# Vision tower: the order of TensorE's small products in the preparation of the state-space scan

## The chip, the cores and the metric

The kernel runs on one core of a Trainium2 chip. The metric is the device time of one execution in microseconds (us), the median of several runs. Engines: PE is TensorE, ACT ScalarE, DVE VectorE, POOL GpSimd, SP SyncE, which here only issues DMAs.

## The reference

An image tokenizer turns 128 images into 5 tokens of 256 channels each (h). Then a bidirectional Mamba block and an expert layer follow. For each of two directions d the Mamba block computes, over the 5 tokens:

```
xz = x @ in_w.T;  xi, z = split(xz)                  # 512 + 512 channels
xc = silu(conv_b + causal 4-tap convolution of xi)
dbl = xc @ xproj_w.T;  dt, Bm, Cm = dbl[:16], dbl[16:32], dbl[32:48]
delta = softplus(dt @ dt_w.T + dt_b)
h = exp(delta * A) * h + delta * Bm * xc;  y = h . Cm    # scan over the tokens
y = (y + xc * D_skip) * silu(z) @ out_w.T
```

## The kernel before, in words

The program is one function, `tower`, in four stages: token, preparation, scan, finish. Each engine has its own list of instructions for each stage, written out by hand; engines meet only at semaphores, so the order of the lists is the order of the work, and a wait holds back all that stands behind it on that engine. The change lies in the preparation alone.

Names on PE in the preparation (128 images on the partitions of a result, or channels where it says so):

- `xi(n)`, n = 0 to 7: input projection of one 128-channel part of a direction (0 to 3 forward, 4 to 7 backward), into PSUM. ACT begins the convolution (`conv_begin`), DVE adds the three other taps, ACT ends it with silu (`conv_end`, semaphore `xc_ready`).
- `xp(d, c)`: the projection `xc @ xproj_w.T`, part c of 4, as 5 products with 48 columns. fp32 products run in two passes, so one `xp` is 10 instructions (L1033). The last part lets ACT copy the result to SBUF (`copy_bc(d)`, tile bct), from which all below follows.
- `turn_dt(d)`: 5 transposes of the dt columns (L1041), then ACT's `copy_dt(d)`.
- `spread_c(d)`: 6 transposes (L1047) of the tile cd, in which POOL has spread the C columns over groups (`c_spread(d)`; the tile is single, so POOL fills it for d = 1 only after `spread_c(0)` has read it), then ACT's `copy_cd(d)`.
- `dt_product(n)`, n = 0 to 9: `dt @ dt_w.T + dt_b` for one (direction, token) item, 33 rows by 512 columns, two passes (L1065). Items 0, 1, 2 are forward; item 3 is the first backward one and needs `copy_dt(1)`. In the text these are the delta products.
- `z(n)`, n = 0 to 7: the gate projection of one item, 128 rows by 512 columns, four passes (L1027). `silu_z(n)` on ACT takes it to SBUF (L1167); n = 0 and 1 are only copied there (their silu follows in the last stage).
- `xt(n)`: 4 transposes and 8 passes of diagonal products (L1056, L1058) for item n.

For each item ACT computes exp(-|.|) (`exponential_of(n)`: L1194, L1199), DVE `plus_one` (L1380), `lost` (L1384) and `above` (L1389), ACT the logarithm (L1210), and DVE then forms delta (`delta_`, L1399), u (L1409), and three bf16 parts of both with ACT (`high` L1219, `middle` L1225, `low` L1433). SP stores these parts in DRAM (`store(n)`, L1012), reads them back for the scan, and between `store(1)` and `store(2)` stores the backward B parts (`store_b(1)`, L1561). Items 0 to 4 run through DVE in a fixed front part (`plus_one` of 2 and 3, `lost` of 2 and 3, `above` of 2 and 3, then item 4, then `delta_(0)`); items 5 to 9 are woven in behind that, one `dt_product(n)` for each, released by `above(n - 1)` (`rc_ready`).

PSUM has 8 banks of 512 columns. Banks 2 and 3 hold in turn the backward `xi(5)`, `turn_dt(0)` and `spread_c(0)`; banks 4 to 7 hold delta and gate products.

Of the kernel before, what the change touches and what calls it, by code (L numbers as in the profile page):

```python
# [76 lines left out]
def tower(nc, a, out):  # L77
    top = ExitStack()
    with top:
# [911 lines left out]
        ZS = [8, 3, 1, 7, 2, 4, 5, 6]  # L991
        Z_BANK = [6, 7, 6, 7, 4, 5, 6, 7]
        NEZ = len(EARLY)
# [21 lines left out]
        def prepare_tensor(pe):  # L1015
# [22 lines left out]
            def turn_dt(d):  # L1038
                pe.wait_ge(bct_ready, d + 1)
                for t in range(L):  # L1040
                    mm = pe.transpose(wide(DTT_SLOT[d], t * B, (t + 1) * B, R), bct[:, d, t, 0:R], ident[:, :])  # L1041
                mm.then_inc(dtt_ready, 1)
# [19 lines left out]
            def dt_product(n):  # L1062
                d, t = ITEMS[n]
                pe.wait_ge(dtT_ready, d + 1)
                pe.matmul(bank(DP_BANK[n]), dtT[:, d, t * B:(t + 1) * B], dtw[:, d, :],  # L1065
                          start=True, stop=True).then_inc(dp_ready, 1)
# [24 lines left out]
            dt_product(0)  # L1091
            pe.wait_ge(acc_ready, 7)
            dt_product(1)
            dt_product(2)
            pe.wait_ge(xc_ready, DC + 3)
            xp(1, 2)
            pe.wait_ge(xc_ready, 2 * DC)
            xp(1, 3)
            spread_c(0)
            pe.wait_ge(acc_ready, 2 * DC)  # L1100
            turn_dt(1)
            dt_product(3)
            pe.wait_ge(rc_ready, 1)
            dt_product(4)
# [12 lines left out]
            pe.wait_ge(CT_ready, 2)  # L1117
            z(0)
            pe.wait_ge(rc_ready, 6)
            dt_product(7)  # L1120
            xt(3)
            z(1)
            pe.wait_ge(rc_ready, 7)
            dt_product(8)
            xt(4)
            pe.wait_ge(z_copied, NEZ + 1)
            z(2)
            pe.wait_ge(rc_ready, 8)
            dt_product(9)
            xt(5)  # L1130
            pe.wait_ge(z_copied, NEZ + 2)
            z(3)
            pe.wait_ge(rc_ready, 9)
# [12 lines left out]
        def prepare_scalar(act):  # L1146
# [100 lines left out]
            conv_end(7)  # L1247
            exponential_of(0)
            copy_bc(1)
            b_high(1)  # L1250
            exponential_of(1)
            copy_dt(1)
            exponential_of(2)
            copy_cd(0)
            exponential_of(3)
            exponential_of(4)
# [12 lines left out]
            middle(2)  # L1269
            silu_z(0, ACT.Copy)  # L1270
            softplus_terms(8)
            high(3)
            middle(3)
            silu_z(1, ACT.Copy)
            softplus_terms(9)
# [1021 lines left out]
```

## Time and profile before

| | |
|---|---|
| median of 3 runs | 502.53 us (500.88 to 507.13) |
| the profiled execution: its own time | 500.95 us |
| its span | 499.1 us |
| mean granted clock of TensorE | 0.965 of full speed |
| PE, DVE, ACT, POOL busy | 90%, 75%, 48%, 34% of the span |

The span runs from the first to the last instruction of the profiled execution; 1.85 us lie around it. A granted clock of 1.00 is 2.4 GHz, 0.50 is 1.2 GHz. The preparation lies at about 204 to 290 us of the span.

### The profile page before, as it was taken

What the parts mean: (1) busy time and instruction counts of PE and PEld (TensorE: products, weight loads), DVE (VectorE), ACT (ScalarE), POOL (GpSimd) and SP (SyncE); (2) the same over time, 40 slices, a digit from 0 to 9 for tenths busy, and PEclk for the clock granted to TensorE, in tenths of its full rate; (3) what the DMA queues carried; (4) which work ended last, traced back from release to release, by engine and by line L of the source; (5) the groups of instructions that cost most, each with busy time, mean ns of one, the idle gap of its engine ahead of it and who ended that gap; (6) DMA issues with size and microseconds to landing.
All of it is one profiled execution on the core that took longest, in us unless ns stands there. A gap on an engine that the chain in (4) does not pass through costs nothing.

```text
span 499.1 us, 6891 instructions
## 1 busy us (share of the span) xinstructions
PE 450.0 (90%) x1816; PEld 228.5 (46%) x1816; DVE 372.3 (75%) x709; ACT 238.8 (48%) x422; POOL 168.4 (34%) x164
## 2 busy tenths in 40 slices
PE   6999999999999989899969738988889889799997
PEld 3554655655555567577635402122222222285654
DVE  0256586566666668564999968899999999989756
ACT  1143423112212323365888855788888888531100
POOL 6000100100100020414430014889898989421000
PEclk9999999999999999996699967899999999999999
DMA  8992029200000000312035663466555655530000
GB/s 262 309 292 80 1 91 304 56 1 0 0 2 0 0 1 0 106 54 80 1 96 174 188 184 83 136 173 193 157 152 173 188 163 158 143 90 12 11 12 21
DMA packets 36344, 51.75 MB, mean 104 GB/s; under 512 B 5922, under 2 KB 26926, under 8 KB 36320
## 3 DMA queue, kind: packets, MB, share of 16 engines
q1 hardware_dynamic: 34736, 49.86, 34.0%
q10 hardware_dynamic: 1584, 1.59, 1.0%
q8 instruction: 12, 0.20, 0.2%
q14 instruction: 12, 0.10, 0.1%
HBM read 34.59 MB, written 16.52 MB: 102 GB/s over the span
## 4 chain that ended last, share of the span: by engine, by line
PE 65%; DVE 10%; SPq 8%; DMA 7%; issue 5%; ACT 3%; POOL 1%; DVEq 0%; POOLq 0%
PE ps L325 14%; PE ps L397 12%; PE ps L2085 7%; PE ps L1730 4%; PE ps L2052 4%; DMA brows<-bparts 4%; PE ps L1020 3%; PE ps L1683 3%; PE ps L1033 2%; DMA area<-in_xT 2%; PE ps L1696 2%; SPq L1544 2%; PE ps L1705 2%; PE ps L346 2%; PE ps L1065 2%
## 5 line engine op out<-in xcount | busy, mean ns | idle before, releaser
L1876 POOL TENSOR_TENSOR gb<-da,hb 128x512 f32<-128x512 f32 x62 | 77.7, 1275 | 61.1 <-ACT da L1796 54.2
L1796 ACT ACTIVATE da<-da 128x512 f32<-128x512 f32 x128 | 79.0, 629 | 25.0 <-DVE da L1907 20.9
L1907 DVE TENSOR_TENSOR da<-ps,expA 128x512 f32<-128x512 f32 x128 | 84.1, 685 | 8.0 <-PE ps L1683 7.2
L325 PE MATMUL ps<-area,convw 128*128 128x384 f32 (+1 forms) x220 | 73.4, 486 | 1.2 <-DMA area<-in_xT 1.2
L397 PE MATMUL ps<-wall,peT 128*128 128x512 f32 x144 | 67.7, 593 | 0.0
L1683 PE MATMUL ps<-drows,selb 96*128 96x512 bf16 x128 | 48.5, 401 | 11.7 <-DVE da L1907 5.1
L325 PEld LDWEIGHTS ps<-area,convw 128*128 128x128 f32 (+1 forms) x220 | 41.2, 190 | 29.0 <-DMA area<-in_xT 1.8
L1696 PE MATMUL ps<-urows,brows 96*128 96x512 bf16 x96 | 35.0, 394 | 13.9 <-DVE gb L1914 7.5
L582 ACT ACTIVATE kvs<-ps 128x512 f32<-128x512 f32 x36 | 21.5, 597 | 52.6 <-PE ps L397 52.6
L574 ACT ACTIVATE peT<-ps 128x384 f32<-128x384 f32 x24 | 11.8, 490 | 66.5 <-PE ps L325 59.3
L1683 PEld LDWEIGHTS ps<-drows,selb 96*128 96x128 bf16 x128 | 11.4, 98 | 61.9 <-DVE da L1907 50.1
L1876 POOL TENSOR_TENSOR gb<-da,gb 128x512 f32<-128x512 f32 x30 | 37.8, 1281 | 0.0
L1730 PE MATMUL ps<-gb,cst 128*8 128x512 f32 x256 | 34.0, 603 | 2.4 <-DVE gb L1969 1.5
L2085 PE MATMUL ps<-expw,xfT 128*128 128x512 f32 x76 | 34.2, 598 | 0.0
L688 DVE BATCH_NORM_STATS2 st<-ps 128x6 f32<-128x256 f32 x40 | 16.8, 429 | 21.7 <-PE ps L346 21.7
L397 PEld LDWEIGHTS ps<-wall,peT 128*128 128x128 f32 x144 | 24.5, 190 | 17.2 <-issue 17.2
L287 POOL TENSOR_TENSOR rstd<-veps,mhalf 128x1 f32<-128x1 f32 x4 | 2.2, 551 | 79.0 <-DVE veps L715 79.0
L1696 PEld LDWEIGHTS ps<-urows,brows 96*128 96x128 bf16 x96 | 9.1, 98 | 35.2 <-DVE gb L1914 21.3
L289 POOL TENSOR_TENSOR rstd<-veps,mhalf 128x9 f32<-128x9 f32 x4 | 7.2, 1806 | 51.5 <-DVE veps L736 51.5
L2178 DVE SCALAR_TENSOR_TENSOR mo<-ps,hot,mo 128x256 f32<-128x256 f32 x40 | 19.3, 484 | 5.5 <-PE ps L2085 4.1
L1914 DVE TENSOR_TENSOR gb<-da,ps 128x512 f32<-128x512 f32 x32 | 21.6, 676 | 1.9 <-ACT da L1796 1.9
L2085 PEld LDWEIGHTS ps<-expw,xfT 128*128 128x128 f32 x76 | 13.9, 190 | 14.8 <-issue 14.1
(246 smaller groups left out, 775.4 us busy)
## 6 DMA issues: line engine op xcount, KB each, us to landing
area<-in_xT SPq DMA_DIRECT2D x11, 768.0 KB
yscr<-yst SPq DMA_DIRECT2D x28, 208.0 KB
brows<-bparts SPq DMA_DIRECT2D x16, 240.0 KB, 3.0
drows<-dparts SPq DMA_DIRECT2D x14, 192.0 KB, 2.8
uparts<-pt SPq DMA_DIRECT2D x18, 128.0 KB, 2.4
dparts<-pt SPq DMA_DIRECT2D x18, 128.0 KB, 2.4
urows<-uparts SPq DMA_DIRECT2D x15, 144.0 KB, 2.7
inw<-in_in_wT SPq DMA_DIRECT2D x2, 1024.0 KB
```

The costliest lines, as they stand in the source:

```text
L325: mm = pe.matmul(bank(T_EMB + j % 2, 0, EN), convw[0:n, k, h * P:(h + 1) * P], xbuf[0:n, q, k, c * EN:(c + 1) * EN], start=(k == 0), stop= ...
L397: mm = pe.matmul(bank(T_KV + (q + t) % 2), peT[:, q, h, t * B:(t + 1) * B], wall[:, h, 512:1024], start=(h == 0), stop=(h == CH - 1))
L582: act.activation(kvs[:, q, t, :], bank(T_KV + (q + t) % 2), ACT.Copy).then_inc(kv_free, 1)
L1683: pe.matmul(bank(j % 2), selb[:, j % 2, :], drows[:, q, o:o + DI], start=True, stop=True).then_inc(e_ready, 1)
L1696: mm = pe.matmul(bank(b_), brows[:, q, o * P:(o + 1) * P], urows[:, q, v:v + DI], start=True, stop=lone, skip_group_check=True)
L1730: mm = pe.matmul(ps[32 * j:32 * j + GB, (6 + k) * 512:(7 + k) * 512], cst[:, q, d, token(s_, d), :], gb_at(q, 4 * k + j), start=True, stop ...
L1796: act.activation(da_at(q, j), da_at(q, j), ACT.Exp, scale=-1.0).then_inc(da_ready, 1)
L1876: pool.tensor_tensor(gb_at(q, j), da_at(q, j), state, ALU.mult).then_inc({2: m2_done, 3: m3_done, 4: m4_done}[s_], 1)
L1907: dve.tensor_tensor(da_at(q, j), bank(j % 2), expA[:, j % 2, :], ALU.mult).then_inc(e_free, 1)
L1914: dve.tensor_tensor(gb_at(q, d), da[:, d, :], bank(bu_bank(q, d)), ALU.mult).then_inc(bu_used, 1)
L2052: mm = pe.matmul(bank(2 + n % 2, 0, C), ygT[:, n % 2, d, c, :], outw[:, d, c, :], start=(d == 0 and c == 0), stop=(d == 1 and c == DC - 1))
L2085: mm = pe.matmul(bank(4 + m % 3), xfT[:, n % 2, h, :], expw[:, h, k * 512:(k + 1) * 512], start=(h == 0), stop=(h == CH - 1))
```

## The change

On PE, `z(0)` comes right behind `dt_product(0)`; the last two parts of the backward projection (`xp(1, 2)`, `xp(1, 3)`) come ahead of `dt_product(1)` and `dt_product(2)`; `turn_dt(1)`, `z(1)`, `dt_product(2)`, `dt_product(3)` follow, and `spread_c(0)`, which stood ahead of `turn_dt(1)`, comes behind them and behind a new wait for the copies of both gate products. These two gate products are written to banks 2 and 3 in place of 6 and 7, and since banks 6 and 7 are free, `z(2)` and `z(3)` take the places of `z(0)` and `z(1)` and lose their waits. On ACT the two copies move forward: behind `exponential_of(0)` and behind `exponential_of(2)`; `copy_cd(0)` moves behind `exponential_of(3)`. The work itself is the same: no instruction is added or removed.

```diff
--- before.py
+++ after.py
@@ -989,7 +989,7 @@
         DP_BANK = [4, 6, 7, 5, 4, 5, 4, 5, 4, 5]
         BC_BANK, DTT_SLOT = [4, 5], [1, 0]
         ZS = [8, 3, 1, 7, 2, 4, 5, 6]
-        Z_BANK = [6, 7, 6, 7, 4, 5, 6, 7]
+        Z_BANK = [2, 3, 6, 7, 4, 5, 6, 7]
         NEZ = len(EARLY)
         XI_AT = [1024 * slot + (NE * B if n < DC else 0) for n, slot in enumerate(XI_SLOT)]
         CD_SLOT = [1, 3]
@@ -1089,17 +1089,20 @@
                 xp(1, c)
             pe.wait_ge(cleared, 3)
             dt_product(0)
-            pe.wait_ge(acc_ready, 7)
-            dt_product(1)
-            dt_product(2)
+            z(0)
             pe.wait_ge(xc_ready, DC + 3)
             xp(1, 2)
             pe.wait_ge(xc_ready, 2 * DC)
             xp(1, 3)
-            spread_c(0)
+            pe.wait_ge(acc_ready, 7)
+            dt_product(1)
             pe.wait_ge(acc_ready, 2 * DC)
             turn_dt(1)
+            z(1)
+            dt_product(2)
             dt_product(3)
+            pe.wait_ge(z_copied, NEZ + 2)
+            spread_c(0)
             pe.wait_ge(rc_ready, 1)
             dt_product(4)
             pe.wait_ge(diag_ready, 2)
@@ -1115,21 +1118,17 @@
             dt_product(6)
             xt(2)
             pe.wait_ge(CT_ready, 2)
-            z(0)
+            z(2)
             pe.wait_ge(rc_ready, 6)
             dt_product(7)
             xt(3)
-            z(1)
+            z(3)
             pe.wait_ge(rc_ready, 7)
             dt_product(8)
             xt(4)
-            pe.wait_ge(z_copied, NEZ + 1)
-            z(2)
             pe.wait_ge(rc_ready, 8)
             dt_product(9)
             xt(5)
-            pe.wait_ge(z_copied, NEZ + 2)
-            z(3)
             pe.wait_ge(rc_ready, 9)
             z(4)
             xt(6)
@@ -1246,13 +1245,15 @@
             b_middle(0)
             conv_end(7)
             exponential_of(0)
+            silu_z(0, ACT.Copy)
             copy_bc(1)
             b_high(1)
             exponential_of(1)
             copy_dt(1)
             exponential_of(2)
+            silu_z(1, ACT.Copy)
+            exponential_of(3)
             copy_cd(0)
-            exponential_of(3)
             exponential_of(4)
             for n in range(5):
                 logarithm(n)
@@ -1267,11 +1268,9 @@
             softplus_terms(7)
             high(2)
             middle(2)
-            silu_z(0, ACT.Copy)
             softplus_terms(8)
             high(3)
             middle(3)
-            silu_z(1, ACT.Copy)
             softplus_terms(9)
             logarithm(5)
             high(4)
```

## Rows read from the trace of the kernel before

**Rows 1.** Page, chain of waits, share of the span by engine.
```profile
PE 65%; DVE 10%; SPq 8%; DMA 7%; issue 5%; ACT 3%; POOL 1%; DVEq 0%; POOLq 0%
```

**Rows 2.** Windows (start:end, length; busy us of each engine; then PEclk, DMA).
```profile
228.00:230.00 2.00, 2.00 (x6) 0.81 (x5) 0.36 (x2) 1.97 (x3) 1.39 (x2) 0.78 0.00 0
...
230.00:232.00 2.00, 2.00 (x12) 2.00 (x11) 1.12 (x2) 0.30 (x1) 0.00 (x0) 0.50 0.47 122
...
244.00:246.00 2.00, 2.00 (x11) 2.00 (x10) 1.93 (x4) 2.00 (x5) 0.00 (x0) 0.50 0.00 0
...
246.00:248.00 2.00, 2.00 (x11) 1.35 (x11) 2.00 (x4) 1.11 (x3) 1.44 (x2) 0.95 0.00 0
```

**Rows 3.** Chain of waits in order of time (start us, us, what), 223 to 241.
```profile
223.97 0.55 PE ps L1041 x5
...
224.51 2.17 PE ps L1033 x20
...
226.68 2.96 PE ps L1065 x6
...
229.64 4.43 PE ps L1033 x20
...
234.07 1.31 PE ps L1047 x6
...
235.38 1.08 PE ps L1041 x5
...
237.22 2.09 PE ps L1065 x2
...
240.63 0.43 DVE rc L1380
```

**Rows 4.** Timeline of ACT (start us, us), 229 to 244.
```profile
229.68 0.63 ACT L1199 ACTIVATE ez<-ez 128x512 f32<-128x512 f32 x1
...
234.10 0.37 ACT L1175 ACTIVATE bct<-ps 128x240 f32<-128x240 f32 x1 [3.80 <-PE ps L1033]
...
241.67 0.63 ACT L1199 ACTIVATE ez<-ez 128x512 f32<-128x512 f32 x1
...
243.61 2.71 ACT L1210 ACTIVATE ez<-ez 128x512 f32<-128x512 f32 x5
```

**Rows 5.** Timeline of DVE, 235 to 246.
```profile
235.96 1.38 DVE L1380 TENSOR_SCALAR rc<-ez 128x512 f32<-128x512 f32 x1 [4.46 <-ACT ez L1199]
...
240.97 1.28 DVE L1384 SCALAR_TENSOR_TENSOR rc<-rc,ez 128x512 f32<-128x512 f32 x2
...
245.15 0.68 DVE L1399 TENSOR_TENSOR du<-rc,ez 128x512 f32<-128x512 f32 x1
```

**Rows 6.** Timeline of POOL at its second spread.
```profile
235.52 1.53 POOL L1335 TENSOR_TENSOR cd<-bct,maskb 128x640 f32<-128x640 f32 x1 [6.14 <-PE ps L1047]
...
237.49 0.46 POOL L1340 TENSOR_TENSOR cd<-cbl,maskb 128x128 f32<-128x128 f32 x1
```

**Rows 7.** Timeline of PE, 246 to 273.
```profile
246.11 0.87 PE L1047 MATMUL ps<-ident,cd 128*128 128x128 f32 x6
...
263.54 1.88 PE L1027 MATMUL ps<-inw,area 128*128 128x512 f32 x4
...
266.40 1.12 PE L1065 MATMUL ps<-dtw,dtT 33*128 33x512 f32 x2 [0.98 <-DVE rc L1389]
...
268.84 3.60 PE L1027 MATMUL ps<-inw,area 128*128 128x512 f32 x8
```

**Rows 8.** Timeline of ACT, 260 to 268.
```profile
260.65 0.58 ACT L1167 ACTIVATE area<-ps 128x512 f32<-128x512 f32 x1
...
267.56 0.60 ACT L1194 ACTIVATE ez<-ps 128x512 f32<-128x512 f32 x1 [1.86 <-PE ps L1065]
```

**Rows 9.** Timeline of DVE at 269.
```profile
269.51 0.69 DVE L1384 SCALAR_TENSOR_TENSOR rc<-rc,ez 128x512 f32<-128x512 f32 x1 [0.24 <-ACT rc L1206]
```

**Rows 10.** Timeline of the SP queue, stores of the second B.
```profile
260.74 1.90 SPq L1561 DMA_DIRECT2D bparts<-bhi  x3
```

## The prediction

> **What bounds the kernel now.** The page's chain of waits comes first: PE has 65% of it, over all stages [rows 1], so only the stretch that the change touches matters. The chain in order of time shows that stretch: from 224 to 239.3 us it is PE nearly throughout (turn_dt, four parts of projection, delta products, spread_c, turn_dt again, dt_product(3)), then one exponential on ACT, and from 240.63 DVE [rows 3]. The windows show why PE takes so long there: its clock is granted in full until about 229 us, is 0.50 (1.2 GHz) in the windows between 229 and 246, and is back at 0.95 in 246:248 [rows 2]. The price is in the chain: the same twenty projection passes take 2.17 us at 224.51 and 4.43 us at 229.64; five transposes take 0.55 and 1.08 us [rows 3]. Behind PE the two others starve: ACT idles 3.80 us before the backward copy_bc, which stands ahead of exponential_of(1) in its list, and DVE idles 4.46 us before plus_one(1) [rows 4, 5]. Before the clock fell, PE had done five narrow transposes, twenty passes of 48 columns and six passes of 33 rows: all small. From 245.15 on DVE works on items in a fixed weave, and everything later hangs on when it starts delta_(0) [rows 5].
>
> **The change part by part.** I count to the end of exponential_of(3), since DVE's lost(2) starts behind plus_one(3) at 240.97 and runs on without a gap to delta_(0) at 245.15 [rows 5]; what that exponential gains, DVE gains.
>
> Prices at the full clock: a delta product occupies PE 0.86 us (a gate product has four passes of 512 columns and a delta product two, so half of what follows; with its tail it shows as 1.12 us [rows 7]). A gate product: one takes 1.88 us with its tail, two take 3.60, so each occupies PE 1.72 us [rows 7]. Two projection parts: 2.17 us. turn_dt 0.55 us. spread_c 0.87 us at 246.11 [rows 3, 7]. ACT: an exponential 1.24 us (0.60 and 0.63), a copy of a gate product 0.58 us [rows 4, 8].
>
> PE, with the clock held at 1.00: dt_product(0) starts at 226.68 and ends at 227.55, z(0) at 229.3, the two projection parts at 231.45, dt_product(1) at 232.3, turn_dt(1) at 232.9, z(1) at 234.6, dt_product(2) and (3) at 236.3.
>
> ACT: exponential_of(0) ends at 230.31 as now, table load included [rows 4]. The copy of z(0) ends at 230.9, in time that was idle: cost nothing, and without that cover 0.6. copy_bc(1) waits for the projection and runs 231.5 to 231.9, against 234.10 now; exponential_of(1), behind dt_product(1), 232.4 to 233.65; copy_dt(1) in the wait that follows; exponential_of(2), for which dt_product(2) is ready at 235.5, to 236.75; the copy of z(1) to 237.35; exponential_of(3) to 238.55. Now it ends at 240.60, at the chain's 240.63 [rows 3]. **Gain 2.05 us.** The copy of z(1) lies on this path, so 0.6 us of what the clock gives back is spent there.
>
> What is late next? The new wait before spread_c(0) holds back, on PE, spread_c(0), dt_product(4) and both first xt. It opens at 237.35, spread_c ends at 238.2, dt_product(4) at 239.1, exponential_of(4) at 240.65 against 242.30 now [rows 4]. DVE needs it only after lost and above of items 2 and 3, at 241.4, so it is covered by 0.8 us. The first logarithm ends 1.9 us behind exponential_of(4) (table load, then the first of the five from 243.61 [rows 4]), thus at 242.55, ahead of delta_(0) at 243.1. POOL's second spread also waits for spread_c(0): now it runs from 235.52 to 237.95 [rows 6], then from 238.3 to 240.75 (with the low clock below, half a microsecond later), while PE reaches spread_c(1) behind two xt at about 241.9. Its later B parts wait for ACT's middle of B, as now, and SP stores them at 260.74 behind store(1) [rows 10]; covered.
>
> The second half is less sure. Between the end of z(1) at 234.6 and the first xt at 239.1 PE has only delta products, a wait of 1.1 us and transposes, the mixture before which the clock fell at 229. I take the clock to be at 0.50 there from about 237.5. Then spread_c takes 1.31 us instead of 0.87, and dt_product(4) 2.09 instead of 1.12 with its tail [rows 3, 7]: 1.4 more. exponential_of(4) ends at about 242.05, 0.65 later than DVE wants it, the first logarithm 1.9 later at 243.95, and delta_(0) starts 0.6 to 0.85 behind 243.1: **a cost of 0.7 us**, bounds 0 (clock held) and 1.4 (both in full on the path). xt(0) and xt(1) at the low clock take as long as now and start earlier.
>
> The trace has the clock return at 246 after two xt, each of them transposes and diagonal products [rows 2], so it can't tell which counted. The Trainium skill, page "TensorE: Matmul & The Clock Gate", section "Part 4: PE-mode transpose", states that transposes do not count as work that brings or keeps the full clock. By that rule the stretch behind z(1) falls to 1.2 GHz, which makes the sum -1.35; if the clock holds there, it is -2.05. No row here shows which.
>
> Moved away from later: z(0) and z(1) and their two copies leave the stretch 252 to 266. There PE waits for DVE (0.98 us before the dt_product at 266.40) and ACT for PE (1.86 us at 267.56), while DVE works almost without a gap [rows 7 to 9]; the 1.72 us of PE and 0.58 of ACT for each [rows 7, 8] free nothing that counts: gain 0. The first of the two dropped waits was open before PE came to it (that copy ended at 261.2, z(2) started at 263.54 [rows 7, 8]), and both gate products now sit behind the same products of DVE: gain 0, bound 0.1. From delta_(0) on, DVE, the last items' ACT work, SP's stores and the loads of the scan follow in the same order, so I take the whole shift through to the end.
>
> Sum: -2.05 + 0.7 = **-1.35 us**. On the profiled execution (span 499.1, 1.85 around it): 500.95 - 1.35 = 499.6 us. Its time lies 1.58 under the median of the runs shown; on the median 502.53 - 1.35 = 501.2 us, my forecast.
>
> **The rivals.**
> 1. *The clock falls at 229 as before* (slower). turn_dt, two projection parts and dt_product(0) stand ahead of z(0) unchanged, 3.6 us of small work, and z(0) may come too late for the clock. Then z(0) has just ended, the projection ends at 233.7 as now, dt_product(1) costs 1.7, turn_dt 1.08, z(1) twice 1.72 = 3.44, so PE is through z(1) only at 239.8. With the clock back by then, dt_product(2), its exponential, the copy and exponential_of(3) end at 240.7, 242.1, 242.65 and 243.9: 3.3 us later than now. Time 502.53 + 3.3 = 505.8. It decides from the point where z(1) runs at 1.2 GHz ahead of delta products that ACT waits for. For it: the fall in the rows follows 5.1 us of small products, and only the last 1.5 of these are replaced. Against it: z(0) has every row and 512 columns, as xi has, beside which the clock stayed up.
> 2. *The clock holds through z(0), but falls during the projection, dt_product(1) and turn_dt that follow* (3.6 us of small work). z(1) then costs up to 1.72 more, and the gain shrinks to -0.3: 502.2.
> 3. *Given back later.* Where z(2) stood at 263.54 PE now idles behind xt(4), some 2.9 us until the next delta product [rows 7]. If the clock falls there, dt_product(9) costs 0.86 more; DVE has a gap of only 0.24 left behind the exponential it feeds [rows 9], and ACT is late with all that follows it. 0.6 to 1.0 us lost: about -0.5, 502.0.
>
> **How the numbers follow.** Forecast 0.45, rival 1 0.2, rival 2 0.2, rival 3 0.15. Low end: both terms at their best (-2.1) on the fastest run shown, 500.88, gives 498.8, and 0.5 less for what one run differs from another. High end: forecast, rivals 2 and 3 on the median reach 502.2; the runs before spread upward by 4.6, and half of rival 1 should be in, so 504.5. A change of 2% would be 10 us, about what this measurement can tell from none; no case comes near half of that: faster 0.01, same 0.97, slower 0.02.
>
> **What the profile after would show.** Clock 1.00 in 228 to 232 and projection passes of about 2.2 us for twenty (right), or 0.50 and 4.4 (rival 1). copy_bc(1) near 231.5. exponential_of(3) near 238.6, delta_(0) near 243.8 instead of 245.15. A clock under 1.00 near 238, but back before dt_product(5). At 260 to 268 a clock of 1.00, else rival 3. The first stores of SP and the scan's first products 1.35 us earlier. Wrong would be: delta_(0) earlier, but the scan's start not; that would mean that stores or loads, not DVE, set the scan's start.

## The result and the profile after

The changed kernel takes 503.89 us (median of 20 runs, 500.52 to 506.39), the kernel before 502.33 us (20 runs, 498.71 to 507.13). The ratio is 1.0046, 95% interval 1.0025 to 1.0067: 1.3 to 3.4 us slower. The forecast was 1.35 us faster. The measured time lies inside the stated range, the direction is wrong.

The profiled execution of the changed kernel took 500.52 us (span 498.7), the fastest of all that were timed, so its span is no measure of the change. What lasts in it is the order of events inside the preparation. I count from the start of plus_one(0) on DVE, which is at 230.34 us before and at 230.04 after. The page's chain of waits of the kernel after, share of the span by engine:

```profile
PE 69%; DVE 13%; issue 8%; ACT 3%; SPq 3%; DMA 2%; POOL 1%; DVEq 1%; POOLq 0%
```

PE leads and DVE follows as in [rows 1], so this page doesn't tell what the change did, and its stretch has to be read by itself. The windows of the kernel after (columns as in [rows 2]):

```profile
228.00:230.00 2.00, 2.00 (x12) 1.28 (x11) 0.10 (x1) 1.97 (x4) 1.10 (x1) 1.00 0.00 0
230.00:232.00 2.00, 2.00 (x16) 1.68 (x15) 1.12 (x2) 0.92 (x4) 0.00 (x0) 1.00 0.59 162
238.00:240.00 2.00, 2.00 (x11) 1.07 (x11) 1.06 (x1) 1.80 (x4) 1.16 (x1) 1.00 0.03 8
240.00:242.00 2.00, 2.00 (x12) 2.00 (x11) 2.00 (x3) 1.95 (x3) 1.92 (x4) 0.51 0.01 4
...
252.00:254.00 2.00, 2.00 (x11) 2.00 (x10) 1.93 (x5) 1.94 (x4) 1.33 (x1) 0.50 0.19 48
```

The clock is at 1.00 where it had fallen in [rows 2], and falls only at 240; in 252:254 it is at 0.50 again. Below, the clock "falls" from 1.00 to 0.50 and "is back" at 1.00. The timeline of PE in the kernel after shows what that gave (a gate product is L1027, a projection part L1033, a delta product L1065 as before; in brackets the idle time ahead and what ended it):

```profile
227.36 1.98 PE L1027 MATMUL ps<-inw,area 128*128 128x512 f32 x4
229.18 2.33 PE L1033 MATMUL ps<-xpw,xcT 128*128 128x48 f32 x20
...
233.04 1.88 PE L1027 MATMUL ps<-inw,area 128*128 128x512 f32 x4
...
251.70 1.12 PE L1056 MATMUL ps<-ident,xcT 128*128 128x128 f32 x4 [4.94 <-DVE area L1423]
...
254.31 3.27 PE L1027 MATMUL ps<-inw,area 128*128 128x512 f32 x4
...
268.13 1.12 PE L1065 MATMUL ps<-dtw,dtT 33*128 33x512 f32 x2 [2.70 <-DVE rc L1388]
```

The timeline of ACT in the kernel after (copy_bc is L1174, the exponential L1198):

```profile
231.54 0.37 ACT L1174 ACTIVATE bct<-ps 128x240 f32<-128x240 f32 x1 [1.05 <-PE ps L1033]
...
238.28 0.63 ACT L1198 ACTIVATE ez<-ez 128x512 f32<-128x512 f32 x1
```

Both early gate products take 1.9 us, z(0) 1.98 and z(1) 1.88, the twenty projection passes 2.33 us with their tail (the slow ones of the kernel before 4.50 in the same view, 4.43 in the chain), and copy_bc(1) runs at 231.54 instead of 234.10 [rows 3, 4]. exponential_of(3) ends at 238.91, 8.9 us behind plus_one(0) instead of 10.3. Up to here the forecast holds, if smaller: 1.4 us. The third gate product, z(2) at 254.31, meets the low clock behind an idle 4.94 us and takes 3.27. The timeline of DVE shows where the 1.4 us went (plus_one L1379, lost L1383, delta_ L1398, rest L1417, the small product of C and B L1374):

```profile
237.31 0.43 DVE L1379 TENSOR_SCALAR rc<-ez 128x512 f32<-128x512 f32 x1 [1.06 <-ACT ez L1198]
238.94 1.71 DVE L1379 TENSOR_SCALAR rc<-ez 128x512 f32<-128x512 f32 x1 [1.21 <-ACT ez L1198]
240.57 1.56 DVE L1383 SCALAR_TENSOR_TENSOR rc<-rc,ez 128x512 f32<-128x512 f32 x2
...
243.25 0.73 DVE L1379 TENSOR_SCALAR rc<-ez 128x512 f32<-128x512 f32 x1
...
245.35 0.68 DVE L1398 TENSOR_TENSOR du<-rc,ez 128x512 f32<-128x512 f32 x1
...
246.67 1.91 DVE L1398 TENSOR_TENSOR du<-rc,ez 128x512 f32<-128x512 f32 x1
248.50 1.89 DVE L1417 TENSOR_TENSOR res<-du 128x512 f32<-128x512 f32 x1
...
252.17 0.23 DVE L1374 TENSOR_TENSOR cbp<-bct 128x80 f32<-128x80 f32 x1
```

plus_one(2) takes 0.43 us, plus_one(3), the same operation on the same shape, 1.71. The two lost take 1.56 together instead of 1.28, plus_one(4) 0.73 instead of 0.41. delta_(1) takes 1.91 and rest(0) 1.89. Beside them stands the timeline of POOL:

```profile
238.84 1.53 POOL L1334 TENSOR_TENSOR cd<-bct,maskb 128x640 f32<-128x640 f32 x1 [9.74 <-PE ps L1047]
...
240.81 0.78 POOL L1339 TENSOR_TENSOR cd<-cbl,maskb 128x128 f32<-128x128 f32 x1
...
246.63 1.40 POOL L1314 TENSOR_TENSOR bmi<-bsmi,maskb 128x640 bf16<-128x640 bf16 x1
247.99 1.85 POOL L1314 TENSOR_TENSOR blo<-bslo,maskb 128x640 bf16<-128x640 bf16 x1
```

POOL's second spread starts at 238.84, 9.74 us after its last work, released by spread_c(0) (L1047) on PE; before it started at 235.52 [rows 6]. plus_one(3) starts 0.1 us after that spread starts and ends 0.28 us after its end: as if it had done its own 0.43 us only once the spread was nearly over. delta_(1) ends 0.55 us behind POOL's B product of 246.63, rest(0) 0.55 us behind the one of 247.99. In the kernel before the same two B products of POOL were there, but fell otherwise. The timeline of DVE in the kernel before:

```profile
246.47 0.68 DVE L1399 TENSOR_TENSOR du<-rc,ez 128x512 f32<-128x512 f32 x1
247.08 0.82 DVE L1418 TENSOR_TENSOR res<-du 128x512 f32<-128x512 f32 x1
...
249.68 1.44 DVE L1375 TENSOR_TENSOR cbp<-bct 128x80 f32<-128x80 f32 x1
```

And the timeline of POOL in the kernel before:

```profile
247.32 1.85 POOL L1315 TENSOR_TENSOR bmi<-bsmi,maskb 128x640 bf16<-128x640 bf16 x1
249.13 1.90 POOL L1315 TENSOR_TENSOR blo<-bslo,maskb 128x640 bf16<-128x640 bf16 x1
```

There delta_(1) ran in 0.68 and rest(0) in 0.82. rest(0) had started ahead of POOL's product, which took 1.85 instead of 1.40: it was the one that waited. Only the small product of C and B was caught, 1.44 us for what takes 0.23 in the kernel after.

Worked out from such rows, for the profiled execution before and three of the changed kernel (the second and third are among the experiments below):

```
us behind the start of plus_one(0)      before   after   second    third
plus_one(3) starts                       10.29    8.90    10.59     8.91
delta_(0) starts                         14.81   15.31    17.47    15.31
delta_(2) starts                         21.09   22.66    23.60    22.67
first product of the scan on PE          56.54   58.59    59.07    58.31
```

The last row is 1.8 to 2.5 us later in all three, about what the ratio says (0.46% of 502, 2.3 us). From delta_(2) to the scan's first product it is 35.45 us before and 35.93, 35.47 and 35.64 in the three. The kernel before has one profiled execution only.

### The profile page after: what moved, and what is told of

It is laid out like the page before. It is cut to its first block, busy times and chain, and to the rows that moved or that the text cites. A ratio compares the mean times of both kernels' runs of the same rounds, so it can differ in the third digit from the quotient of the medians.

```text
span 498.7 us, 6892 instructions
## 1 busy us (share of the span) xinstructions
PE 447.1 (90%) x1816; PEld 226.2 (45%) x1816; DVE 373.3 (75%) x709; ACT 239.1 (48%) x422; POOL 168.0 (34%) x164
## 4 chain that ended last, share of the span: by engine, by line
PE 69%; DVE 13%; issue 8%; ACT 3%; SPq 3%; DMA 2%; POOL 1%; DVEq 1%; POOLq 0%
PE ps L325 14%; PE ps L397 12%; PE ps L2084 7%; PE ps L1682 4%; PE ps L1729 4%; PE ps L2051 4%; DVE da L1906 3%; PE ps L1020 3%; PE ps L1695 2%; PE ps L1704 2%; PE ps L1033 2%; PE ps L308 2%; PE ps L346 2%; PE ps L1713 1%; PE ps L1027 1%
## 5 line engine op out<-in xcount | busy, mean ns | idle before, releaser
L397 PEld LDWEIGHTS ps<-wall,peT 128*128 128x128 f32 x144 | 24.5, 190 | 17.2 <-issue 17.2
```

Of the source, the lines that this page charges most:

```text
L397: mm = pe.matmul(bank(T_KV + (q + t) % 2), peT[:, q, h, t * B:(t + 1) * B], wall[:, h, 512:1024], start=(h == 0), stop=(h == CH - 1))
```

## The experiments

Theory 1: POOL's second spread, moved later by the new place of spread_c(0), holds up DVE operations and shifts the later B products against DVE too. Theory 2: the new falls of the clock (at 240 and from 250 to 257 us, around TensorE's idle 4.94 us) cost the time. All ratios are to the kernel before, with 95% intervals. "Scan" is the first product of the scan behind the start of plus_one(0): 56.54 before, 58.59 after.

**Two buffers for the spread C, changed kernel.** Only POOL's wait goes away.

```diff
-                if d == 1:
-                    pool.wait_ge(cdT_ready, 1)
+                cd = cds[d]
...
+            pool.wait_ge(cdT_ready, 1)
             for q in range(2):
                 pool.memset(drows[0:KS // 2, q, :], 0.0).then_inc(cleared, 1)
```

cds[0] lies in a tile that is not in use at that time; PE's transposes read the buffer of their direction. The wait is back where POOL's clearing comes, behind both spreads.

> The changed kernel with a second buffer for the spread C columns, so that POOL's second spread starts when the backward columns are copied (near 232 us) instead of behind spread_c(0) (238.84 us). Theory 1 (POOL's spread holds up DVE's plus_one of item 3, 1.71 us instead of 0.43, and what follows): plus_one(3) takes about 0.43 us, delta_(0) starts near 243.5 instead of 245.35 us; the B parts of POOL still meet delta_(1) and rest(0), so those may stay long; time 1.5 to 2 us under the changed kernel, at the kernel before or up to 1 us under it. Theory 2 (the clock near 240 us and the late gate product at 254 us cost the time): no change of delta_(0), time as the changed kernel.

Measured: 0.9991 (0.9968 to 1.0015), 501.31 us. The interval lies wholly under that of the changed kernel (1.0025 to 1.0067). Timeline of DVE in this kernel:

```profile
240.38 0.43 DVE L1379 TENSOR_SCALAR rc<-ez 128x512 f32<-128x512 f32 x1 [1.21 <-ACT ez L1199]
...
246.24 0.69 DVE L1398 TENSOR_TENSOR du<-rc,ez 128x512 f32<-128x512 f32 x1
246.84 0.83 DVE L1417 TENSOR_TENSOR res<-du 128x512 f32<-128x512 f32 x1
...
249.45 1.44 DVE L1374 TENSOR_TENSOR cbp<-bct 128x80 f32<-128x80 f32 x1
```

Timeline of POOL in this kernel:

```profile
233.44 1.53 POOL L1334 TENSOR_TENSOR cd<-bct,maskb 128x640 f32<-128x640 f32 x1 [2.90 <-ACT bct L1175]
```

Timeline of PE in this kernel, the first transposes of xt(2):

```profile
248.98 0.66 PE L1057 MATMUL ps<-ident,xcT 128*128 128x128 f32 x4 [0.78 <-DVE area L1423]
```

plus_one(3) is back to 0.43, delta_(1) and rest(0) to 0.69 and 0.83; the small product of C and B is caught instead (1.44), as before. plus_one(0) starts at 231.48 here, so delta_(0) comes at 13.44 and delta_(2) at 19.72, scan at 55.18. With TensorE's list unchanged, some 2.8 us come back (1.0046 - 0.9991 of 502; 1.2 to 4.4 by the two intervals, an estimate); expected were 1.5 to 2. The clock's fall at 10.0 us behind plus_one(0) is here too, so that one isn't what was lost. The second fall is gone, and with it the idle time ahead of xt(2), 0.78 us instead of 4.94. By then delta_(2) is already 2.94 us earlier than in the profile after (19.72, 22.66), of 3.41 at the scan, so at most 0.5 us is the second fall's.

**POOL's spread late, kernel before.** The loss without TensorE's new order.

```diff
                 if d == 1:
                     pool.wait_ge(cdT_ready, 1)
+                    pool.wait_ge(ez_ready, 3)
```

> The kernel before, with one thing added: POOL's second spread waits for the third exponential (near 238.3 us instead of 235.5 us), where DVE begins its unbroken run. TensorE's order is that of the kernel before. Theory 1: plus_one(2) or (3) takes over 1 us, delta_(0) starts 0.7 to 1.7 us later than 245.15 us, time 0.7 to 2 us over the kernel before. Theory 2 (all of the loss comes from TensorE's new order): time as the kernel before, delta_(0) within 0.2 us of 245.15.

Measured: 1.0029 (0.9997 to 1.0062); delta_(0) at 16.32, 1.5 us later than before, scan at 59.31, 2.8 us later. Timeline of DVE in this kernel:

```profile
241.29 2.63 DVE L1385 SCALAR_TENSOR_TENSOR rc<-rc,ez 128x512 f32<-128x512 f32 x2
...
248.15 1.91 DVE L1400 TENSOR_TENSOR du<-rc,ez 128x512 f32<-128x512 f32 x1
```

Timeline of POOL in this kernel:

```profile
238.71 1.68 POOL L1336 TENSOR_TENSOR cd<-bct,maskb 128x640 f32<-128x640 f32 x1 [9.15 <-ACT ez L1199]
...
241.53 1.85 POOL L1315 TENSOR_TENSOR bhi<-bshi,maskb 128x640 bf16<-128x640 bf16 x1
```

Not plus_one but the two lost were caught (2.63 us instead of 1.28), and delta_(1) and rest(0) as in the changed kernel. The place was expected wrongly, the mechanism and the size in the trace are theory 1's. TensorE idles 4.12 us ahead of xt(2) here, and the clock falls at 19.2 us behind plus_one(0): theory 2's second fall, in the old order too. The time's interval just touches 1, so here the trace, not the time, carries the reading.

**All of POOL's second half early, changed kernel.** Two buffers, and ACT's middle of the backward B behind copy_dt(1).

```diff
             copy_dt(1)
+            b_middle(1)
...
-            b_middle(1)
             high(0)
```

> As the kernel with two buffers, and ACT's middle of the backward B columns comes right behind copy_dt(1), so that POOL's two large B products (1.4 us each) run before 240 us instead of beside delta_(1) and rest(0). Theory 1: delta_(1) and rest(0) take 0.68 and 0.8 us instead of 1.91 and 1.89; plus_one(3) may wait up to 0.9 us for the last of them; delta_(2) starts at 249 to 249.5 us against 252.70 in the changed kernel and 251.43 in the one before; time 2 to 2.5 us under the kernel before, 4 under the changed one. Theory 2: delta_(2) moves by under 0.5 us, time as the changed kernel.

Measured: 0.9999 (0.9965 to 1.0034). delta_(1) and rest(0) took 0.69 and 0.68 as expected, but delta_(2) came at 20.04, not at 19.0 to 19.5 (the expectation's 249 to 249.5, less 230.04). plus_one(2) and plus_one(3) were caught by the early B products instead (1.17 and 1.08). The clock fell at 7.4 us behind plus_one(0), just ahead of spread_c(0), and dt_product(4) and its exponential came late; and plus_one(4) met another of POOL's works. Timeline of DVE in this kernel:

```profile
245.67 1.10 DVE L1379 TENSOR_SCALAR rc<-ez 128x512 f32<-128x512 f32 x1 [0.27 <-ACT ez L1199]
```

Timeline of POOL in this kernel:

```profile
242.66 3.82 POOL L1858 MEMSET drows<- 48x2048 bf16 x2
```

plus_one(4) took 1.10 us beside the clearing of drows, which only writes. The two lost and two above during the same clearing took 1.28 for two, undisturbed. The scan came at 56.45, and of that 0.95 us was lost far behind: the clock fell at 34.7, in the idle time ahead of dt_product(9). Timeline of PE in this kernel:

```profile
268.03 2.07 PE L1066 MATMUL ps<-dtw,dtT 33*128 33x512 f32 x2 [2.70 <-DVE rc L1388]
```

It takes 2.07 us instead of 1.12, and from delta_(4) to delta_(5) it is 11.36 us instead of 10.41 before.

**The same, with the clearing held.**

```diff
+            pool.wait_ge(rc_ready, 5)
             for q in range(2):
                 pool.memset(drows[0:KS // 2, q, :], 0.0).then_inc(cleared, 1)
```

> As the changed kernel with two buffers and the early B parts, and POOL's clearing of drows (3.82 us, ending inside DVE's plus_one of item 4, which took 1.10 us) held until the fifth rc is done. Theory 1: plus_one(4) takes 0.43 us, delta_(2) starts at 18.5 to 19.5 us behind plus_one(0) if the clock holds until dt_product(4), at 19.5 to 20 if it falls before; time 1 to 2 us under the kernel before.

Measured: 0.9976 (0.9951 to 1.0002), 500.61 us, the lowest ratio of all, and under the changed kernel's interval; against the kernel before it isn't settled. plus_one(4) took 0.41 as expected, but delta_(2) came at 20.68, not at 18.5 to 20. The profiled execution shows the first half of what rival 1 described. Its timeline of PE:

```profile
227.64 3.25 PE L1028 MATMUL ps<-inw,area 128*128 128x512 f32 x4
```

The clock fell during z(0), which took 3.25 us instead of 1.98; plus_one(1) started at 5.53 instead of 3.85, plus_one(3) at 10.58; the clock was back by z(1), which is where it parts from rival 1. It fell again at 35.4, ahead of dt_product(9), with the same 0.97 us lost as in the kernel just shown. Scan at 57.09.

**In addition delta product 4 ahead of spread_c(0).**

```diff
-            pe.wait_ge(z_copied, NEZ + 2)
-            spread_c(0)
             pe.wait_ge(rc_ready, 1)
             dt_product(4)
+            pe.wait_ge(z_copied, NEZ + 2)
+            spread_c(0)
```

(and exponential_of(4) ahead of copy_cd(0) on ACT.)

> As the last one, and dt_product(4) goes ahead of the wait and of spread_c(0), its exponential ahead of copy_cd(0): item 4 no longer depends on whether the clock falls near spread_c(0). plus_one(4) waits for nothing; delta_(0) at 13 to 13.5 us and delta_(2) at 18 to 19 us behind plus_one(0); time 1.5 to 2.5 us under the kernel before, and the fastest of all.

Measured: 0.9995 (0.9968 to 1.0023); not the fastest. In its profile the clock fell at -2.7, 4.2 and 11.0 us behind plus_one(0), so both gate products ran partly slow, and plus_one(3) came only at 12.27, delta_(2) at 21.72 instead of the expected 18 to 19. The reordering can't be judged from that profile.

**POOL's second half early, kernel before.** Two buffers, ACT's middle of B early and the clearing held, with TensorE's old order: the two edits on ACT and POOL that are shown for the kernels above, and

```diff
-                if d == 1:
-                    pool.wait_ge(cdT_ready, 1)
+                cd = cds[d]
```

> The kernel before with TensorE's old order, and of the rest only what was given to POOL's side: two buffers for the spread C, the middle of the backward B right behind copy_dt(1), and POOL's clearing of drows held until the fifth rc is done. Intervals counted from the start of plus_one(0). Theory 1 (contention of POOL and DVE is worth as much as TensorE's order): plus_one(3) starts as before at 10.3 us, delta_(0) at 14 to 15.5 (14.81 before), delta_(2) at 20 to 20.5 (21.09 before); time 0.5 to 1 us under the kernel before. The difference to the same changes on the new order (the next kernel but one) is what TensorE's new order is worth once POOL is out of the way: 1 to 1.5 us.

Measured: 1.0033 (1.0010 to 1.0056): slower, where 0.5 to 1 us faster was expected. In the trace plus_one(3) at 10.31 took 1.52 beside a B product that now fell there, so that delta_(0) came at 15.94, later than the expected 14 to 15.5; delta_(2) at 20.86 and scan at 56.50 were as before. That profile explains no loss, so the cause of this ratio stays open.

**Only the order of the small products.** Gate products and their copies stay where they were before.

```diff
             dt_product(0)
-            pe.wait_ge(acc_ready, 7)
-            dt_product(1)
-            dt_product(2)
             pe.wait_ge(xc_ready, DC + 3)
             xp(1, 2)
             pe.wait_ge(xc_ready, 2 * DC)
             xp(1, 3)
-            spread_c(0)
+            pe.wait_ge(acc_ready, 7)
+            dt_product(1)
             pe.wait_ge(acc_ready, 2 * DC)
             turn_dt(1)
+            dt_product(2)
             dt_product(3)
+            spread_c(0)
```

(and copy_cd(0) behind exponential_of(3) on ACT.)

> The new order of the small products alone: projection ahead of delta products 1 and 2, spread_c(0) last, the gate products and their copies where they were before. If the gate products hold the clock: the clock falls near 229 us as before, exponential_of(3) ends at 240 us or later against 238.9 in the changed kernel, delta_(0) no earlier than 246 us, time 1 to 3 us over the kernel before. If the order alone holds it: clock 1.00 to about 235 us, exponential_of(3) near 236 to 237 us, since 3.4 us of gate products are gone from the path.

Measured: 0.9985 (0.9959 to 1.0012), where 1 to 3 us slower was expected. The clock fell at -2.0 us, as expected, and still plus_one(3) started at 9.46, earlier than before (10.29): what the low clock costs is nearly made up by the 3.4 us of gate products that aren't in the way (9.46 against 8.90 in the changed kernel). POOL's spread caught the two lost (2.64 us), its B products plus_one(4) (1.13) and rest(0) (1.90), so delta_(0) came at 16.08 and scan at 57.67. The trace is 1.1 us behind the kernel before, the median is not; one execution need not have the clock of most.

**The same with two buffers.** POOL's edit of the first experiment on top of this order:

```diff
-                if d == 1:
-                    pool.wait_ge(cdT_ready, 1)
+                cd = cds[d]
```

> The new order of the small products without early gate products (0.9985 of the kernel before; lost took 2.64 us for two there, rest(0) 1.90), with two buffers for the spread C. Theory 1: without POOL's late spread delta_(0) comes 1.5 to 2 us earlier than there (14.1 to 14.6 us behind plus_one(0) instead of 16.08), the first scan product at 55.5 to 56.3 us instead of 57.67; time 0.996 to 0.999.

Measured: 1.0015 (0.9986 to 1.0045), just above what was expected. In the trace delta_(0) at 13.23, scan at 55.09, even earlier than expected.

**Two buffers alone on the kernel before.** POOL's edit as in the two-buffer experiment on the changed kernel, and no other; TensorE's and ACT's lists are those of before.

> The kernel before with two buffers for the spread C and nothing else. Together with the changed kernel with two buffers (0.9991, first scan product 55.18 us behind plus_one(0)) it gives the worth of TensorE's new order with POOL out of its way. Theory 1 (the order is worth its 1.4 us, POOL took more than that back): POOL's spread starts 1 us earlier than before (at about 4.2 us behind plus_one(0)), the run of DVE from plus_one(3) at 10.3 us is as before, the first scan product at 56 to 56.8 us, time 0.9975 to 1.001 of the kernel before. If this one is faster than 0.997, two buffers alone are the gain and the order is worth nothing.

Measured: 0.9991 (0.9962 to 1.0020), scan at 55.64, both against 0.9991 and 55.18 of the changed kernel with them. So with POOL's spread out of the way TensorE's new order is worth 0.5 us in the traces and nothing that the times show; the two intervals leave room for some 1.9 us either way (an estimate). In this execution of the old order the clock fell only at -0.1 us behind plus_one(0), where it was -1.2 in the profile before, and plus_one(3) came at 9.37 instead of the 10.3 of the three other executions with that order.

**The small product of C and B early, changed kernel with two buffers.** DVE does it behind above(1), where it is idle.

```diff
             above(1)
+            dot = c_dot_b(1)
...
                 if n == 0:
-                    ch.upto(c_dot_b(1))
+                    ch.upto(dot)
```

> The changed kernel with two buffers, and DVE's small product of C and B of the second direction (1.44 us behind POOL's last B product, 0.23 alone) in DVE's idle time ahead of plus_one(2). Theory 1: the B product of POOL then holds up delta_(2) in its place, so delta_(2) comes only 0.3 to 0.6 us earlier than 19.72 us behind plus_one(0), first scan product at 54.7 us; time 0.996 to 0.999 of the kernel before. If it comes 1.4 us earlier, POOL's hold falls on nothing that counts.

Measured: 1.0015 (0.9981 to 1.0048), no gain. Timeline of DVE in this kernel:

```profile
240.34 0.23 DVE L1374 TENSOR_TENSOR cbp<-bct 128x80 f32<-128x80 f32 x1
...
252.35 1.89 DVE L1398 TENSOR_TENSOR du<-rc,ez 128x512 f32<-128x512 f32 x1
```

Timeline of POOL in this kernel:

```profile
251.84 1.85 POOL L1315 TENSOR_TENSOR blo<-bslo,maskb 128x640 bf16<-128x640 bf16 x1
```

The small product takes 0.23 now, and delta_(2) takes 1.89 in its place, as theory 1 expected: it starts at 19.24, 0.5 earlier, and ends 1.2 later than it would alone. The clock fell at 7.4 here and item 4 came late by it, and the scan is at 55.90.

**z(2) behind delta product 7, changed kernel.** For theory 2: this takes the slow gate product from in front of dt_product(7).

```diff
-            z(2)
             pe.wait_ge(rc_ready, 6)
             dt_product(7)
             xt(3)
+            z(2)
```

> The changed kernel with the gate product z(2) behind dt_product(7) and xt(3). Theory 1: the late, slow gate product at 254 us costs at most the 0.5 us by which the stretch from delta_(2) to the first scan product is longer than before (35.93 against 35.45 us); delta_(0) and delta_(2) don't move (15.3 and 22.7 us behind plus_one(0)); time as the changed kernel, 0 to 0.5 us less. Theory 2 (the second fall of the clock, at 250 to 257 us, is what the change costs): time back to that of the kernel before, 1.5 to 2 us under the changed one.

Measured: 1.0134 (1.0115 to 1.0153), five runs, 6.7 us slower than the kernel before and 4.4 slower than the changed one. Neither theory expected that. delta_(0) and delta_(2) were at 15.32 and 22.67 as in the changed kernel; the loss is behind them, scan at 63.46. Timeline of PE in this kernel:

```profile
254.47 1.11 PE L1056 MATMUL ps<-ident,xcT 128*128 128x128 f32 x4 [5.08 <-DVE area L1423]
...
260.04 2.04 PE L1065 MATMUL ps<-dtw,dtT 33*128 33x512 f32 x2 [2.74 <-issue]
...
264.62 4.97 PE L1027 MATMUL ps<-inw,area 128*128 128x512 f32 x8
269.52 1.12 PE L1065 MATMUL ps<-dtw,dtT 33*128 33x512 f32 x2
```

The clock fell at 17.5 us behind plus_one(0), in the idle 5.08 us, and came back only at 34.6; two gate products in a row at the low clock (4.97 us) put dt_product(8) off to 269.52, and DVE stood idle for 2.1 and 2.4 us for u(3) and u(4), which need xt(3) and xt(4). In the profile after, with z(2) ahead of dt_product(7), it was back at 27.1. The loss is that of the order and of the low clock together: the two gate products in a row would take 3.60 at the full clock [rows 7], and what each share is, isn't separated.

**z(2) ahead of xt(2), changed kernel.** It fills the idle time.

```diff
             dt_product(6)
-            xt(2)
             pe.wait_ge(CT_ready, 2)
             z(2)
+            xt(2)
```

(and copy_cd(1) ahead of high(0) on ACT.)

> The changed kernel with the gate product z(2) ahead of xt(2), in the 4.94 us in which TensorE stands idle, and ACT's copy_cd(1), which it needs, ahead of high(0). POOL is untouched. Theory 1 (POOL holds up DVE): delta_(0) near 15.3 and delta_(2) near 22.7 to 23 us behind plus_one(0) as in the changed kernel; the clock may hold past 20 us; time at most 0.5 us under the changed kernel. Theory 2 (the fall of the clock in that idle time is what costs): the stretch from delta_(2) to the first scan product back to 35.5 us and the time down to that of the kernel before, 1.5 us or more under the changed one.

Measured: 1.0049 (1.0016 to 1.0081), as the changed kernel; delta_(0) at 15.33, delta_(2) at 22.68. Timeline of PE in this kernel:

```profile
249.20 3.61 PE L1027 MATMUL ps<-inw,area 128*128 128x512 f32 x4 [0.40 <-ACT CT L1179]
...
259.24 1.70 PE L1065 MATMUL ps<-dtw,dtT 33*128 33x512 f32 x2 [3.80 <-DVE rc L1388]
```

The clock still fell at 17.2, was back at 20.6, and the idle time has only moved: 3.80 us now stand before dt_product(7), the clock fell again at 27.4, and that product, xt(3) and the next gate product (3.38 us) ran slow. Scan at 60.37; this execution (506.99 us) is the slowest of its eight. Theory 2's gain didn't come, but the test isn't clean, since it made a new gap.

**Both: two buffers and z(2) ahead.** The edit just shown, with that of the first experiment:

```diff
+                cd = cds[d]          # POOL
...
-            xt(2)                    # PE
             pe.wait_ge(CT_ready, 2)
             z(2)
+            xt(2)
```

> The kernel with two buffers for the spread C and in addition z(2) ahead of xt(2) with its copy ahead of high(0). If both causes count, this is the fastest: delta_(2) near 19.7 us behind plus_one(0), no fall of the clock between 15 and 30 us, time 1 to 2.5 us under the kernel before. If only POOL counts, it times as the kernel with two buffers alone (0.9991 of the kernel before).

Measured: 1.0066 (1.0035 to 1.0097), where the fastest of all or at least 0.9991 was expected. delta_(2) at 19.71 as expected, and then dt_product(7) behind 4.81 us of idle at the low clock, delta_(4) at 32.39 instead of 30.38, scan at 57.40. As in the kernel with z(2) ahead alone, the new gap cost more than the filled one.

**The changed kernel twice more, one profiled execution each.**

> The changed kernel once more, for a second profiled execution: its profiled one (500.52 us) is the fastest of 20, so it may not be typical. If the clock's fall comes at another moment from one execution to the next, this one shows z(0) or z(1) partly at 1.2 GHz (3.2 us instead of 1.9) and delta_(0) 1 to 3 us later than 15.3 us behind plus_one(0), or a longer low stretch around 250 us. If it falls at a fixed place in the order, the intervals repeat within 0.1 us. plus_one(3) or an operation near it is held up by POOL either way.

> The changed kernel once more, as the last one; same expectations.

The third execution (503.51 us in all) repeats the profile after to 0.02 us up to delta_(2). In the second (502.02 us) the clock fell at 2.6 us behind plus_one(0), during turn_dt(1). Timeline of PE in this second execution:

```profile
234.08 3.23 PE L1027 MATMUL ps<-inw,area 128*128 128x512 f32 x4
```

Timeline of DVE in this second execution:

```profile
241.67 2.61 DVE L1383 SCALAR_TENSOR_TENSOR rc<-rc,ez 128x512 f32<-128x512 f32 x2
...
245.41 1.44 DVE L1379 TENSOR_SCALAR rc<-ez 128x512 f32<-128x512 f32 x1
...
250.13 1.89 DVE L1417 TENSOR_TENSOR res<-du 128x512 f32<-128x512 f32 x1
```

z(1) takes 3.23 instead of 1.88, plus_one(3) starts at 10.59: the whole gain of TensorE is gone, as rival 2 had it (its price was 1.72 us, here it is 1.69). POOL still takes its toll, only from others: the two lost 2.61, plus_one(4) 1.44, rest(0) 1.89.

## Why the prediction was wrong

**What bounds the kernel** was read rightly: exponential_of(3) moved, and DVE's run started with it.

**The gain of 2.05 us** was there but smaller: plus_one(3) came 1.4 us earlier in two of the three executions of the changed kernel and 0.3 later in one. Over all eleven executions with this order of small and gate products it came at 8.9 in eight, and at 10.6, 10.6 and 12.3 in three in which z(0) or z(1) ran partly at the low clock, against 10.3 before. The mis-sized term is PE's sum: dt_product(2) was ready for ACT 5.97 us behind plus_one(0), where the sum gave 5.2. It took 0.86 us for a delta product and 1.72 for a gate product, which is what they cost among their own kind; ahead of another kind of product they held PE for 1.05 (dt_product(1), 231.44 to 232.49) and 1.81 (z(1), 233.04 to 234.85), and ACT can start only behind the tail of dt_product(2), which the sum left out. With two delta and two gate products ahead of it these make the 0.8 us.

**The step that failed is "What is late next?"**, and in it the sentence that POOL's second spread, now from 238.3, is covered. I asked who waits for POOL's data, and that was right (spread_c(1) came in time). I didn't ask who runs beside POOL. [rows 5] held the warning: plus_one(1) at 235.96 took 1.38 us, plus_one(3) 0.43 at 240.63 [rows 3], the same operation, and POOL's spread of [rows 6] stood beside the first. The forecast's own times had the spread at 238.3 to 240.75 and DVE's unbroken run beginning at 238.55. In the kernel before the hold fell on a DVE that still waited for ACT, with 0.26 us of idle time left ahead of plus_one(3); the change moved the same spread from 5.2 to 8.8 us behind plus_one(0), into that run. Measured there: +1.28 on plus_one(3), +0.28 on the two lost, +0.32 on plus_one(4), together 1.88, so delta_(0) came 0.5 us later instead of 1.35 earlier.

**"I take the whole shift through to the end"** failed for the same reason: behind delta_(0), POOL's two B products caught delta_(1) and rest(0) (+1.23 and +1.07) and no longer the small product of C and B (-1.21), another 1.1 us. Between delta_(2) and the scan come 0 to 0.5 us more. In the profile after, these stand between delta_(2) and delta_(4) (11.12 us instead of 10.67), where xt(2), the gate product at 254.31 and xt(3) come late; from delta_(5) to the scan it is 14.4 in all these executions.

**The cost of 0.7 us for the low clock behind z(1)**: the clock fell at 8.9 to 10 us behind plus_one(0) in the profile after and in the third execution, about 2 us later than taken, and exponential_of(4) wasn't late for DVE, which POOL had already delayed. The term wasn't needed there; in the kernel with POOL's work early it did cost what was feared (dt_product(4) late, exponential_of(4) 1.6 us later). Nor must the clock fall in this stretch: in the three kernels with z(2) moved, whose order up to there is the same, it held through spread_c(0), dt_product(4) and the first two xt, until 17.2, 17.5 and 24.3. The prediction's choice between -1.35 and -2.05 has no one answer.

**The rivals.** The clock of rivals 1 and 2 was seen, in some executions of the same order, not in others. Rival 3 was placed rightly and is a matter of chance too. In all eleven executions in which z(2) has left its place PE idles 2.70 us ahead of dt_product(9), instead of 0.98 in the six in which it hasn't. In the profile after the clock held there and the product at 268.13 took its 1.12, as in [rows 7]. In eight of the eleven the clock fell in that idle time or behind it, in none of the six. Behind dt_product(9), as in the second and third execution (at 40.2 and 39.6), the fall cost the scan nothing. It came ahead of that product in three: in the two kernels with POOL's B work early that were shown above it cost 0.95 and 0.97 us, where the prediction had 0.6 to 1.0, and in the kernel with z(2) pushed back its share isn't separated. So rival 3 took nothing in the three profiles of the changed kernel and isn't what made it slower. None of the three rivals had POOL in it; the slower side of the forecast stood on the clock alone, so that the measured time lies inside the range is luck.

**What is shown and what not.** Shown: with the same list on TensorE, POOL's spread out of the way brings the time from 1.0046 back to 0.9991, and the spread put late into the old order gives the same kind of long DVE operations and a scan 2.8 us later. With two buffers old and new order can't be told apart by their times (0.9991 both). Open: why the old order with POOL's B work early is slower (1.0033), and how often the clock falls early; the profiles are single executions.

The clock's second fall goes with a late DVE, whatever made it late. It comes with TensorE's idle time ahead of xt(2), which waits for DVE's skip (L1423). In seven executions that idle time was 1.92, 2.56, 2.62, 2.66, 3.32, 4.12 and 4.94 us, and the clock fell between 19.2 and 23.1 us behind plus_one(0) in each of them, under the old order (2.66, 4.12) as under the new. In the kernel before and in six others, all with two buffers for the spread C, it was at most 1.27 us, and the clock held there. Idle time alone doesn't settle it: at other places of the same executions the clock held through 1.7 to 2.0 us of it, and in two of them ahead of dt_product(9) through 2.70. Nor is it always POOL's spread that made DVE late: the 1.92 and the 2.66 stand in kernels with two buffers, where the clock's earlier falls and a B product did it. The second fall's own share, up to 0.5 us, isn't measured by itself, since both tests of it made gaps of their own.

One kernel, two buffers with the early B work and the held clearing, beats the changed one (0.9976, interval 0.9951 to 1.0002, against 1.0025 to 1.0067); whether it beats the one before isn't settled.

## What to carry to other kernels

When an operation is moved or released later on one engine, list not only who needs its result but what runs beside it on DVE and POOL at the new place: the same DVE operation with two clearly different durations in one trace is the sign. A single buffer between POOL and TensorE ties POOL's timing to TensorE's order; a second buffer cut that tie here and cost no time (0.9991 in the old order too). And filling a gap on TensorE by pulling work forward opens a gap where it stood: one gate product pulled forward ahead of xt(2) gained nothing (1.0049), and pushed back behind xt(3) it cost 4.4 us more (1.0134 against 1.0046).

## What the runs showed of the hardware

POOL and DVE hold each other up, each until the other's operation has about ended. How long a held operation takes can be told beforehand: in every trace here a caught tensor_scalar of 128x512 ended 0.27 to 0.29 us behind POOL's operation (29 cases), a caught one with two SBUF inputs and 512 columns 0.54 to 0.56 behind it (34 cases). Caught were on DVE: tensor_scalar from SBUF to SBUF (0.43 alone, 1.71 beside the spread, 1.10 beside a clearing that only writes) and operations with two SBUF inputs (delta_ 0.68 and 1.91, rest 0.68 and 1.89, two lost 1.28 and 2.64), the latter not beside the clearing. Never caught were those with an input from PSUM (above 0.64 to 0.69, u 0.67 to 0.69 in every trace, some 15 of each beside a POOL operation that reads SBUF). POOL is caught in turn (a B product 1.40 alone and 1.85 behind a DVE operation). The Trainium skill, page "SBUF — State Buffer", section "Who interferes with whom", states this division: DVE operations with two SBUF inputs contend with POOL operations that read SBUF, tensor_scalar in its two-port mode with any, and whoever starts first holds the other for the whole instruction. By that rule each row above is as it should be, and the trace agrees, with the one addition that the held DVE operation shows as long, not as waiting: plus_one(3) is 1.71 us of busy time, and nothing of the hold is in the idle times.

The granted clock falls at different moments of one and the same order: in the eleven executions that have the new order up to delta_(0) nearly or fully in common, it fell first at -2.7, -2.1, 2.6, 7.4, 7.4, 8.9, 10.0, 10.0, 17.2, 17.5 and 24.3 us behind plus_one(0) (read from windows of 1 us). A chain built on its staying up is a matter of chance for each execution.
